# Edge-attention stage of a two-layer graph network: indicator matrices made on ScalarE from squared distances, and sums that alternate between two PSUM banks

## The reference

```
h   = relu(layernorm(x))                       # 3125 x 256
q, k, v = split(layernorm(h) @ Wqkv + bqkv)    # 8 heads of 32
scores = sum(q[src] * k[dst], per head)        # one per edge and head
e   = exp(scores - max over the edges of dst)
agg = segment_sum(v[src] * e, dst) / segment_sum(e, dst)
x1  = h + agg
x   = x + x1 + gelu(layernorm(x1) @ W_in + b_in) @ W_out + b_out
h   = relu(layernorm(x))
h_all = h @ W[r] for 8 relations               # 25000 x 256
x   = x + layernorm(gelu(segment_sum(h_all[src, type], dst) + h @ loop_w + h_bias + h)) * gamma + beta
```

## Time and profile before

| | |
|---|---|
| median of 3 runs | 1514.89 us (1512.42 to 1517.97) |
| the profiled execution | 1513.77 us, of which the span of the profile is 1511.9 us |
| TensorE busy | 1178.1 us, 78% |
| VectorE busy | 908.2 us, 60% |
| GpSimd busy | 896.2 us, 59% |
| ScalarE busy | 459.8 us, 30% |

### The profile page before, as it was taken

How to read it: one execution, slowest core, us unless ns; L and a number is a source line. 1 busy time by engine, 2 the same in 40 slices (tenths; PEclk the granted TensorE clock), 3 DMA queues, 4 the chain that set the end, 5 groups by cost and what they waited for, 6 DMA issues and landing times. The chain is left out here.

```text
span 1511.9 us, 18542 instructions
## 1 busy us (share of the span) xinstructions
PE 1178.1 (78%) x5460; PEld 854.6 (57%) x5460; DVE 908.2 (60%) x2797; ACT 459.8 (30%) x1150; POOL 896.2 (59%) x960
## 2 busy tenths in 40 slices
PE   5875779999899999899999897677666666666663
PEld 2442667777677777677777765444444444444441
DVE  5664877767777767777777774213444443444443
ACT  5553234454444453444443443200000000000000
POOL 1655767555555555555555540077777777777770
PEclk9997999999999999999999999967888888888885
DMA  6548867676666666666666641134444444444441
GB/s 211 145 129 265 261 210 238 213 233 207 213 202 206 222 223 200 211 194 191 223 209 197 214 131 67 60 115 128 127 132 130 128 129 132 133 125 131 130 131 34
DMA packets 136570, 256.31 MB, mean 170 GB/s; under 512 B 40390, under 2 KB 85424, under 8 KB 133266
## 3 DMA queue, kind: packets, MB, share of 16 engines
q0 software_dynamic: 50176, 154.19, 33.5%
q1 hardware_dynamic: 85330, 99.71, 20.7%
q10 hardware_dynamic: 960, 1.18, 0.2%
HBM read 192.76 MB, written 62.25 MB: 169 GB/s over the span
## 5 line engine op out<-in xcount | busy, mean ns | idle before, releaser
L1039 POOL DMA_INDIRECT arena<-qv_tab,srcs x392 | 397.7, 1015 | 299.5 <-PE ps L1226 214.4
L1606 POOL DMA_INDIRECT arena<-h_all,typs x392 | 377.0, 962 | 132.8 <-issue 131.3
L1669 PE MATMUL ps<-arena 128*128 128x256 f32 x784 | 280.0, 493 | 174.6 <-DMA arena<-h_all,typs 171.5
L1669 PEld LDWEIGHTS ps<-arena 128*128 128x128 f32 x784 | 169.8, 238 | 272.1 <-DMA arena<-h_all,typs 218.0
L1226 PE MATMUL ps<-arena 128*128 128x264 f32 x784 | 217.8, 401 | 73.5 <-DVE arena L1368 73.1
L1226 PEld LDWEIGHTS ps<-arena 128*128 128x128 f32 x784 | 137.8, 191 | 124.5 <-DVE arena L1368 95.0
L1429 DVE TENSOR_TENSOR arena<-arena,ps 128x512 f32<-128x512 f32 x196 | 134.3, 685 | 104.2 <-PE ps L1215 94.7
L1278 PE MATMUL ps<-wrel,arena 128*128 128x512 f32 x400 | 188.1, 596 | 1.4 <-ACT arena L1126 1.4
L1215 PE MATMUL ps<-arena 128*128 128x264 bf16 x1176 | 167.8, 280 | 18.3 <-DVE arena L1352 16.7
L1215 PEld LDWEIGHTS ps<-arena 128*128 128x128 bf16 x1176 | 144.1, 145 | 46.4 <-DVE arena L1352 17.1
L1620 ACT ACTIVATE arena<-ps 128x256 f32<-128x256 f32 x49 | 18.8, 384 | 426.7 <-PE ps L1681 407.5
(11 more groups left out here) (150 smaller groups left out, 1399.6 us busy)
## 6 DMA issues: line engine op xcount, KB each, us to landing
h_all<-arena SPq DMA_DIRECT2D x25, 1024.0 KB, 6.0
arena<-dst SPq DMA_DIRECT2D x49, 256.0 KB, 4.4
rel<-arena SPq DMA_DIRECT2D x77, 128.0 KB, 2.3
arena<-k_tab SPq DMA_DIRECT2D x49, 198.0 KB, 2.8
att<-arena SPq DMA_DIRECT2D x52, 132.0 KB, 2.8
qv_tab<-arena SPq DMA_DIRECT2D x25, 256.0 KB, 3.0
arena<-qv_tab,srcs POOLq DMA_INDIRECT x392, 4.3
arena<-h_all,typs POOLq DMA_INDIRECT x392, 2.8
```

The costliest lines, as they stand in the source:

```text
L1039: pool.indirect_dma_start(out=rowbuf[:, u * T + t, 0:2 * D], out_offset=None, in_=qv_tab, in_offset=bass.IndirectOffsetOnAxis(ap=srcs[:, v ...
L1606: pool.indirect_dma_start(out=rowbuf[:, u * T + t, :], out_offset=None, in_=h_all, in_offset=bass.IndirectOffsetOnAxis(ap=typs[:, v * T + ...
L1669: last = nc.tensor.matmul(ps[:, 6 + u, 0:D], ind[:, u, t, :], rowbuf[:, u * T + t, :], start=(t == 0), stop=(v == 0 and t == T - 1))
```

## The change

`turn` and its PSUM bank go. ScalarE makes `ind` itself: for each of the 8 tiles it squares the distance between the column number and the edge's place in the window (`distances(v, half)`, 4 tiles in a call), and then relu(1 - 2 * square) gives 1 where the distance is 0 and 0 elsewhere (`indicators(v, half)`, on 4 tiles at once, in place). The offsets of all edges (`ndl`) and a column of ones are made once by VectorE at the start. `take`, `add_up` and `carry` use bank 4 or 5 by the parity of v, and `add_up(v, 0)` waits for the take of v - 2 instead of v - 1. The first visit's indicators are made ahead of the loop; the others are spread over the previous visit in four pieces.

```diff
+            ndl = cut([G, T])
+            ones = cut([1])
...
-            TURN, AGG = 4, 5
+
+            def bank_a(v):
+                return 4 + v % 2
...
-                def indicators(v):
-                    act.wait_ge(turn_ready, v + 1)
+                def distances(v, half):
                     if v >= 2:
                         act.wait_ge(agg_done, PAIRS * (v - 1))
-                    for half in range(2):
-                        nc.scalar.activation(ind[:, v % 2, 4 * half:4 * half + 4, :],
-                                             ps[:, TURN, half * 2 * WIN:(half + 1) * 2 * WIN].bitcast(BF16).rearrange("p (t w) -> p t w", w=WIN),
-                                             ACT.Copy).then_inc(ind_ready, 1)
+                    for t in range(4 * half, 4 * half + 4):
+                        last = nc.scalar.activation(ind[:, v % 2, t, :], iotaj[:, :], ACT.Square, bias=ndl[:, v, t:t + 1])
+                    last.then_inc(squares, 1)
+
+                def indicators(v, half):
+                    act.wait_ge(squares, 2 * v + half + 1)
+                    i = ind[:, v % 2, 4 * half:4 * half + 4, :]
+                    nc.scalar.activation(i, i, ACT.Relu, bias=ones[:, :], scale=-2.0).then_inc(ind_ready, 1)
...
-                indicators(0)
+                act.wait_ge(offsets_ready, 2)
+                for half in range(2):
+                    distances(0, half)
+                    indicators(0, half)
...
                     weights(v, 1)
                     if old is not None:
                         keep_messages(old, 1)
+                    if more:
+                        distances(v + 1, 0)
+                    if old is not None:
                         keep_messages(old, 2)
+                    if more:
+                        indicators(v + 1, 0)
+                        if old is not None:
+                            distances(v + 1, 1)
                     weights(v, 2)
                     if old is not None:
                         keep_messages(old, 3)
+                    elif more:
+                        distances(v + 1, 1)
                     if hid is not None:
                         weights(v, 3)
                         y_features(hid)
-                    if v + 1 < G:
-                        indicators(v + 1)
+                    if more:
+                        indicators(v + 1, 1)
...
-                def turn(v):
-
-                    if v >= 1:
-                        pe.wait_ge(ind_ready, 2 * v)
-                    tiles = indT[:, v % 2, :].rearrange("p (e t) -> p t e", t=T)
-                    for t in range(T):
-                        last = nc.tensor.transpose(ps[:, TURN, t * WIN // 2:(t + 1) * WIN // 2].bitcast(BF16),
-                                                   tiles[:, t, :], identb[:, :])
-                    last.then_inc(turn_ready, 1)
...
-                    if j == 0 and v >= 1:
-                        pe.wait_ge(osum_ready, v)
+                    if j == 0 and v >= 2:
+                        pe.wait_ge(osum_ready, v - 1)
...
-                turn(0)
...
-                    if v + 1 < G:
-                        turn(v + 1)
...
+                nc.vector.memset(ones, 1.0).then_inc(offsets_ready, 1)
+                nc.vector.tensor_tensor(ndl, wst[:, :].unsqueeze(2).broadcast_to([128, G, T]),
+                                        dstf[:, :].rearrange("p (g t) -> p g t", t=T), ALU.subtract).then_inc(offsets_ready, 1)
```

More of the change, by code:

```diff
@@ L713, in program @@
             indT_ready, car_ready = sem("indT_ready"), sem("car_ready")
-            turn_ready, ind_ready = sem("turn_ready"), sem("ind_ready")
+            offsets_ready, squares, ind_ready = sem("offsets_ready"), sem("squares_ready"), sem("ind_ready")
             exp_done, w_ready, agg_done = sem("exp_done"), sem("weighted_ready"), sem("summed")
@@ L1081, in take @@
                         act.wait_ge(att_out, 16 * (v - 1))
-                    nc.scalar.activation(osum[:, v % 2, :], ps[:, AGG, 0:AW], ACT.Copy).then_inc(osum_ready, 1)
-                def indicators(v):
-                    act.wait_ge(turn_ready, v + 1)
+                    nc.scalar.activation(osum[:, v % 2, :], ps[:, bank_a(v), 0:AW], ACT.Copy).then_inc(osum_ready, 1)
+                def distances(v, half):
                     if v >= 2:
                         act.wait_ge(agg_done, PAIRS * (v - 1))
-                    for half in range(2):
-                        nc.scalar.activation(ind[:, v % 2, 4 * half:4 * half + 4, :],
-                                             ps[:, TURN, half * 2 * WIN:(half + 1) * 2 * WIN].bitcast(BF16).rearrange("p (t w) -> p t w", w=WIN),
-                                             ACT.Copy).then_inc(ind_ready, 1)
+                    for t in range(4 * half, 4 * half + 4):
[5 more added lines that the diff above has]
+                    nc.scalar.activation(i, i, ACT.Relu, bias=ones[:, :], scale=-2.0).then_inc(ind_ready, 1)
                 def weights(v, j):
@@ L1134, in keep_messages @@
                                          ACT.Copy).then_inc(msg_taken, 1)
-                indicators(0)
+                act.wait_ge(offsets_ready, 2)
+                for half in range(2):
+                    distances(0, half)
+                    indicators(0, half)
                 for v in range(G):
                     hid, out, old = hid_of(v), out_of(v), before(v)
+                    more = v + 1 < G
                     if v == FIRST:
@@ L1222, in add_up @@
                     pe.wait_ge(ind_ready, 2 * v + j // 2 + 1)
-                    if j == 0 and v >= 1:
-                        pe.wait_ge(osum_ready, v)
+                    if j == 0 and v >= 2:
+                        pe.wait_ge(osum_ready, v - 1)
                     for t in (2 * j, 2 * j + 1):
-                        last = nc.tensor.matmul(ps[:, AGG, 0:AW], ind[:, v % 2, t, :], rowbuf[:, v % 2 * T + t, D:2 * D + H],
+                        last = nc.tensor.matmul(ps[:, bank_a(v), 0:AW], ind[:, v % 2, t, :], rowbuf[:, v % 2 * T + t, D:2 * D + H],
                                                 start=(t == 0), stop=(v == 0 and t == T - 1))
@@ L1237, in carry @@
                     pe.wait_ge(car_ready, v)
-                    nc.tensor.matmul(ps[:, AGG, 0:AW], car[:, v % 2, :], osum[:, 1 - v % 2, :], start=False, stop=True).then_inc(win_done, 1)
+                    nc.tensor.matmul(ps[:, bank_a(v), 0:AW], car[:, v % 2, :], osum[:, 1 - v % 2, :], start=False, stop=True).then_inc(win_done, 1)
                 def turn_y(m):
```

## The result

| | before | after |
|---|---|---|
| median | 1515.60 us (1512.42 to 1517.97, 4 runs) | 1527.89 us (1525.93 to 1529.71, 4 runs) |
| span of the profiled execution | 1511.9 us | 1524.1 us |

The ratio is 1.0083, with a 95% interval of 1.0062 to 1.0105: the changed kernel is 12.3 us slower. The forecast was 6 us faster, with a range up to 1516. The forecast was wrong.

The account below looks back on a forecast made before the run. TensorE was taken to bound the hid half, VectorE the out half. Gains of 22 x 0.27 = 5.9 us, plus 0.3 in the first visit, made 1513.77 - 6.2 = 1507.6; the median, 1.12 higher, 1508.7 us; range 1502 to 1516.

Parts of the forecast that it names:

- What bounds the kernel: Fused stage, period 32.29 us: VectorE sets the pace in the out half, TensorE in the hid half.
- The hid turn: Hid half: removing 0.66 us of transposes gains 0.27 us per period, as hidden then waits for y_features; 22 visits, 5.9 us.
- The out turn: Out half: removing 0.65 us of transposes is worth 0; TensorE's wait for VectorE grows from 1.67 to about 2.3 us.
- rival D: TensorE's clock falls behind the longer out-half wait, 1.6 us lost per period, +29 us, 1544 us; chance 0.08.
- C: Rival: ScalarE's queue delays the messages; squares of 0.8 us each would add 13 us, 1528 us; chance 0.05.
- ScalarE's work: Both halves: squares of 0.29 us and relus of 0.7 add 5 us per period, fitting ScalarE's gaps; worth 0.
- Two banks: add_up(v, 0) waits for an older take; TensorE is nowhere seen to wait for take, so worth 0.
- The start and the third block: Offsets and visit 0's indicators lie beside the gathers, worth 0, bounds -1 and +1; the third block stays unchanged.

Follow-up runs that it names:

- e7: The changed kernel with 8 unused transposes put back on TensorE in both out and hid visits from v = 4 on; 1515.28 us, ratio 1.0006.
- e1: The changed kernel with 8 unused transposes put back on TensorE in the out visits alone, where the turn stood; 1509.63 us, ratio 0.9960.
- e2: The kernel before with squares and relus only in the hid visits, turn and copies elsewhere, bank 5 alone for the sums; 1509.52 us, ratio 0.9975.
- e5: The kernel before with turn(v + 1) moved ahead of add_up(v, 1) on TensorE in the out visits; 1537.06 us, ratio 1.0156.
- e8: e2 with, in the hid visits, turn_y ahead of keys(v + 1, 0) on TensorE and y_features ahead of the last weights on ScalarE; 1504.24 us, ratio 0.9933.
- e9: The changed kernel with 6 unused transposes on TensorE in the out visits, where the turn stood; 1507.13 us, ratio 0.9956.
- e6: The changed kernel with 4 unused transposes on TensorE in the out visits, where the turn stood; 1526.48 us, ratio 1.0097.
- e3: The kernel before with squares and relus only in the out visits, turn and copies elsewhere, bank 5 alone for the sums; 1536.08 us, ratio 1.0142.
- e4: The changed kernel with VectorE's scale_of moved one pair later, behind the scores of pair 3 of the out visit; 1518.44 us, ratio 1.0019.
- e10: e4 with 8 unused transposes on TensorE ahead of turn_h1 in the out visits; 1507.38 us, ratio 0.9945.

## Why the prediction was wrong, point by point

**What bounds the kernel: right.** The out half goes by VectorE and the hid half by TensorE; e7 and the periods of 32.00 us confirm it.

**The hid turn, 0.27 us: right** (0.28). The last hid visit, which had no turn, was the row to read: it gave the gain that busy time (0.66) would have overstated more than twofold.

**The out turn, "Worth 0": this is the step that failed.** The cover was there: VectorE's chain is untouched, and the wait grew, to 2.16 us (estimated 2.3; the 8 transposes, 0.65 us in the rows, had shortened it by 0.49). But the transposes did two things. They made tiles, and they kept TensorE at work ahead of a wait. The second was booked only under rival D and given 0.08. The measured price of the step is 13 x 1.39 = 18 us over the 20 regular periods, and 18 us again when e1 puts the work back.

**Rival D, why its chance was too low.** The mechanism was named, with its place. Its size was overstated, in two terms that lie on the same side: a fall in each of 22 periods (in the 20 regular ones 13 came), and 1.6 us a fall (1.39 measured); hence 1544 where 1527.9 came. The chance rested on one row: a wait of 1.98 us in the earlier trace rows, behind which the clock stayed at 1.00. I read it as "1.98 is safe". After the change a wait of 2.16 us left the clock up in 7 periods of 20 as well, so a single wait without a fall shows little: the same wait at the same place gives both outcomes. The row that counted was the other one: the longest regular wait, 1.67 us in the earlier trace rows, was the longest length known to be borne in every period, and the change went beyond it 22 times. The number by itself would have named the wrong rival: 1527.9 is what C gave (1528, for squares of 0.8 us), but the squares took 0.316 us, and e7 shows no delay from them. That C's number came out is chance.

**ScalarE's work: right in place, a little off in size.** The squares took 0.316 us each (taken: 0.29, bound 0.454), the relu 0.72 (taken: 0.7). Four squares took 1.26 us, and e7 shows that nothing is delayed. The Trainium skill, "ScalarE: Activation LUTs", section "What ACT_TABLE_LOAD costs", gives a time for an ACTIVATE with a bias from memory and an overlap of neighbours; the estimate from it was 387 ns for such a square by itself and 1.27 us for four. The trace agrees, with 388 ns and 1.26 us.

**Two banks, worth 0: right.** e2 does without them and runs as fast as e1.

**The start and the third block: right.** From `turn_y` of the last hid visit to the end of the span are 1524.1 - 926.78 = 597.3 us, before 1511.9 - 913.35 = 598.6.

**The range** was built around the forecast, and D lay outside it on the grounds of its 0.08. A mechanism that acts in each of 22 periods, whose only evidence against was one row, should have widened it.

## What to carry to other kernels

Before work is taken off TensorE in front of a wait, look at what the wait becomes. If it grows past the longest one that the trace shows to be borne regularly at full clock, the gain can turn into a loss several times as large (here 5 to 6 us against 18), since the slow clock is then paid in the half that TensorE bounds. Take work from the half where the engine is the bound and leave it where it only fills; and if a long wait cannot be avoided, a few matmuls that nobody reads are cheap there (e1 against the changed kernel: 18 us gained; 8 were enough and 4 were not). The order of such work within one engine's wait matters as much as its amount (e5: 22 us for a move).

## What the runs showed of the hardware

The waits of TensorE in the out half, and in how many of 20 regular periods the granted clock fell from 1.00 (2.4 GHz) to 0.50 (1.2 GHz):

| kernel | waits in the out half, us | falls |
|---|---|---|
| before, e1, e2, e7, e8 | 1.01 or 1.02, 1.66 or 1.67 | 0 |
| e9 | 1.01, 1.79 | 0 |
| e6 | 1.01, 1.91 | 12 |
| the changed kernel | 1.02, 2.16 | 13 |
| e3 | 1.01, 2.15 | 15 |
| e5 | 0.52, 2.16 | 15 |
| e4 | 1.02, 0.17, 1.53, 0.25 | 7 |
| e10 | 1.01, 0.17, 1.05, 0.25 | 0 |

Neither the longest wait nor the sum orders these rows (e4 against the kernel before, e5 against the kernel before). How the waits lie to one another and to the work between them matters, and by which rule is left open here. Two things were not expected: that 0.12 us at this place separates no fall from 12 (across two chips, see e9), and that a wait repeated to the hundredth of a microsecond brings the clock down in some periods and not in others, so that a kernel of equal periods gets periods of two lengths.

The falls are not scattered at random. These are the 1.4 us behind the wait of 2.16 us in six out visits of the changed kernel that follow one another; the lower the granted clock of the stretch, the earlier the fall in it:

```profile
583.40:584.80 1.40, 1.40 (x4) 1.13 (x5) 1.40 (x5) 0.31 (x1) 0.00 (x0) 0.60 0.73 237
616.80:618.20 1.40, 1.40 (x7) 1.18 (x8) 1.40 (x5) 0.31 (x1) 0.00 (x0) 0.86 0.74 214
650.20:651.60 1.40, 1.40 (x8) 1.22 (x9) 1.40 (x5) 0.31 (x1) 0.00 (x0) 1.00 0.80 249
682.20:683.60 1.40, 1.40 (x4) 1.06 (x5) 1.40 (x5) 0.31 (x1) 0.00 (x0) 0.67 0.70 208
715.60:717.00 1.40, 1.40 (x7) 1.20 (x8) 1.40 (x5) 0.31 (x1) 0.00 (x0) 0.93 0.77 214
749.00:750.40 1.40, 1.40 (x8) 1.22 (x9) 1.40 (x5) 0.31 (x1) 0.00 (x0) 1.00 0.80 240
```

With 1.00 before a fall and 0.50 after it, 0.60 puts the fall some 0.3 us behind the wait, 0.86 some 1.0 us; then one period has none, and it begins again with 0.67 (0.5 us) and 0.93 (1.2 us). So the place of the fall drifts against the kernel's own period. Where the wait lies in time seems to count beside its length; no run tested that.

The Trainium skill, "TensorE: Matmul & The Clock Gate", Part 1, describes the halving of the clock as the consequence of idle time. The trace agrees as to the two levels. It does not need one long idle stretch, though: in e4 the clock fell with no wait above 1.54 us in the out half. Nor does TensorE's busy time around the waits tell which period gets a fall. In the changed kernel it is 7.23 us of 10.40 in a period without a fall and in the next one, at the end of which the clock falls:

```profile
640.80:651.20 10.40, 7.23 (x41) 5.91 (x41) 8.31 (x27) 5.20 (x14) 4.80 (x5) 1.00 0.68 207
672.80:683.20 10.40, 7.23 (x39) 5.91 (x39) 8.31 (x27) 5.21 (x14) 4.81 (x5) 0.97 0.70 205
```
